# A decoder stack on one core: the barrier between the third feed-forward and the last self attention, and which engine casts the cross attention's keys

## The reference, cut to what matters

```python
x = x + _L2_ffn_ref(_layernorm(x), gate_w, gate_b, val_w, val_b, out_w, out_b)   # three bit_linear
x = x + _L3_attn_ref(_layernorm(x), w_qkv, b_qkv, w_out, b_out)                  # 16 heads of 16, causal
x = x + _L3_xattn_ref(_layernorm(x), ctx, mask, wq, bq, wk, bk, wv, bv, wo, bo)  # 16 heads of 16, int8 q and out
x = x + _L3_ffn_ref(_layernorm(x), ...)                                          # 7 experts, top 3, and a shared one

def bit_linear(x, w, b):
    scale_x = 127.0 / clip(max(abs(x), -1), 1e-5)
    x_dq = clip(round(x * scale_x), -128, 127) / scale_x
    gamma_w = clip(mean(abs(w)), 1e-5)
    return x_dq @ (clip(round(w / gamma_w), -1, 1) * gamma_w).T + b
# l2 ffn: bit_linear(silu(bit_linear(x, gate)) * bit_linear(x, val), out)
```

## Time and profile before

| | us |
|---|---|
| median of 3 runs | 1626.39 |
| lowest, highest | 1625.09, 1630.17 |
| the profiled execution | 1614.99 |
| its span | 1613.7 |
| PE busy, share of the span | 1374.7, 85% |
| DVE | 1080.9, 67% |
| ACT | 791.3, 49% |
| POOL | 757.0, 47% |

### The profile page before, as it was taken

How to read it: one execution, slowest core, us unless ns; L and a number is a source line. 1 busy time by engine, 2 the same in 40 slices (tenths; PEclk the granted TensorE clock), 3 DMA queues, 4 the chain that set the end, 5 groups by cost and what they waited for, 6 DMA issues and landing times. The chain is left out here.

```text
span 1613.7 us, 26001 instructions
## 1 busy us (share of the span) xinstructions
PE 1374.7 (85%) x8488; PEld 1038.5 (64%) x8488; DVE 1080.9 (67%) x2767; ACT 791.3 (49%) x2003; POOL 757.0 (47%) x1226
## 2 busy tenths in 40 slices
PE   6999997889999996777799698556888878889999
PEld 4666763578888872444477587424666655568887
DVE  7877786357767668898955736676766688853222
ACT  3444442144334357888821624456767668742111
POOL 4888882046666565777722122335556533320000
PEclk9999997999999998999999899869999999999999
DMA  8000001100000016656550000020423246310000
GB/s 291 15 8 8 1 1 68 56 15 8 1 8 1 1 11 127 111 100 108 102 209 1 0 1 0 4 111 14 66 50 57 43 96 168 75 14 1 7 8 13
DMA packets 177285, 79.98 MB, mean 50 GB/s; under 512 B 165376, under 2 KB 169856, under 8 KB 176000
## 3 DMA queue, kind: packets, MB, share of 16 engines
q1 hardware_dynamic: 177152, 78.33, 21.0%
HBM read 37.40 MB, written 1.05 MB: 24 GB/s over the span
## 5 line engine op out<-in xcount | busy, mean ns | idle before, releaser
L101 PE MATMUL banks<-normed_t,arena_a 128*128 128x256 f32 x1120 | 257.1, 385 | 2.5 <-PEq L3685 2.5
L464 POOL TENSOR_TENSOR lut_weights<-lut_weights,arena_b 128x536 f32<-128x536 f32 x128 | 181.3, 1417 | 123.6 <-DVE arena_b L454 114.4
L101 PEld LDWEIGHTS banks<-normed_t,arena_a 128*128 128x128 f32 x1120 | 215.2, 193 | 33.0 <-issue 3.1
L601 POOL TENSOR_SCALAR work<-work,small 128x256 f32<-128x256 f32 (+1 forms) x384 | 175.6, 475 | 37.1 <-DVE small L593 37.1
L1752 ACT ACTIVATE arena_a<-banks,work 128x1024 uint8<-128x1024 f32 x128 | 153.8, 1204 | 34.0 <-DVE work L1692 22.0
L1690 DVE TENSOR_REDUCE work<-banks 128x1 f32<-128x1024 f32 x128 | 155.5, 1215 | 11.8 <-PE banks L101 11.6
L1797 POOL TENSOR_SCALAR arena_a<-arena_a 128x1024 bf16<-128x1024 uint8 x128 | 132.4, 1045 | 57.4 <-DMA arena_a<-arena_a 54.9
L107 PE MATMUL banks<-identity,work 128*128 128x128 f32 x1000 | 140.0, 282 | 18.8 <-POOL work L601 7.2
L581 ACT ACTIVATE work<-banks,small 128x256 f32<-128x256 f32 (+1 forms) x258 | 114.8, 453 | 67.6 <-DVE small L568 55.4
L107 PEld LDWEIGHTS banks<-identity,work 128*128 128x128 f32 x1000 | 116.9, 145 | 41.6 <-issue 17.8
L1916 DVE TENSOR_TENSOR big_b<-big_b,banks 128x512 f32<-128x512 f32 (+2 forms) x48 | 30.8, 642 | 135.0 <-PE banks L101 122.8
(11 more groups left out here) (467 smaller groups left out, 3193.7 us busy)
## 6 DMA issues: line engine op xcount, KB each, us to landing
arena_a<-in_L3f_wg SPq DMA_DIRECT2D x8, 512.0 KB, 3.9
arena_b<-in_lut_idx SPq DMA_DIRECT2D x8, 268.0 KB, 3.3
arena_b<-in_L_wqn SPq DMA_DIRECT2D x4, 512.0 KB, 8.6
arena_b<-in_L_wo SPq DMA_DIRECT2D x4, 512.0 KB, 12.5
arena_a<-in_L_wq SPq DMA_DIRECT2D x1, 2048.0 KB, 7.5
arena_a<-in_L_wo SPq DMA_DIRECT2D x1, 2048.0 KB, 12.6
arena_a<-arena_a SPq DMA_TRANSPOSE x128, 2.5
arena_b<-in_L2f_gv SPq DMA_DIRECT2D x1, 2048.0 KB, 7.9
```

What stands on the lines that cost most here:

```text
L101: ins = t.matmul(out, lhs_t, rhs, start=start and i == 0, stop=stop and i == n - 1)
L464: g.tensor_tensor(o, o, lut_t[j % 2], ALU.add).then_inc(*summed.up(c * LUT + j))
L601: ins = g.tensor_scalar(e[:, c], e[:, c], A.rl[n % 2][:, 2 * hh + i:2 * hh + i + 1], 0.0, ALU.mult, ALU.add)
```

## The change

- `l2_ffn` has no meeting at its end. Steps 0 and 1 of self attention are issued in its steps 9 and 10, behind each engine's own work of the step; the common loop starts at step 2. `l3_attention()` is called once ahead of all stages.
- POOL's work behind the feed-forward's loop (masks, identity, fills, scaling) is issued in steps 3, 4 and 6; the value tiles' memsets in steps 6 and 8, three each.
- Batch 3's norm moves from steps 0 and 1 of self attention to step 5 (POOL), 6 (ACT) and 7 (PE's turn, ACT's copy).
- In place of the barrier there are waits: PE for the scaled weights and the last silu before projection 0, and before each score bank's first use; ACT for the last down product before the first exponentials, and for hidden tile 6 before the first query casts; DVE for hidden tile 7 before the first key casts.
- In cross attention POOL makes all the key casts (`key_parts_gpsimd`): the first behind the queries' bias, the second behind the rests of the first, both ahead of its own wait for ACT's cast, and the third at the start of the next even step, ahead of the next queries' bias. Self attention's key casts stay on DVE.

```diff
@@ exponentials_scalar
+            elif A.before:
+                a.wait_ge(*(yield A.before))
@@ l2_ffn, tensor (vector, scalar alike, in the loop over n)
-            yield MEET
+                if n >= NT + 1:
+                    yield from self_tensor(n - NT - 1)
@@ l2_ffn, gpsimd
-            for r in above:
-                g.memset(r, 0.0).then_inc(*gs.up())
...
-            yield MEET
+                if n == 3:
+                    for r in above:
+                        g.memset(r, 0.0).then_inc(*gs.up())
...
+                if n == 4:
+                    g.tensor_scalar(id_100, id_b, 100.0, 0.0, ALU.mult, ALU.add).then_inc(*gs.up())
...
+                if n == 6:
+                    g.wait_ge(*(yield loaded[9], "all"))
...
+                    gs.all("l3a", "scaled")
+                if n in (6, 8):
+                    half = narrow_vs[0:3] if n == 6 else narrow_vs[3:6]
+                    for r in half:
+                        g.memset(r, 0.0).then_inc(*gs.up())
...
+                if n >= NT + 1:
+                    yield from self_gpsimd(n - NT - 1)
@@ parts_vector, parts_scalar
+        if N is self_n and m < 2 and n == 0:
+            v.wait_ge(*(yield gs, "l2f", "hidden", NT - 1))
...
+        if N is self_n and m < 2 and n == 0:
+            a.wait_ge(*(yield h_in_psum, "l2f", NT - 2, 1))
+            a.wait_ge(*(yield gs, "l2f", "hidden", NT - 2))
@@ new
+    def key_parts_gpsimd(N, m, n):
+        cur, k5 = N.current(m, n), slots(N.kx[m % 2])
+        ks = K_SLOTS[n]
+        if n == 0:
+            g.wait_ge(*(yield vs, N.A.s, "keys", m))
+        else:
+            g.wait_ge(*rest_of.now())
+        for i in range(TB):
+            src = cur[:, i, 64:128].rearrange("p (h o c) -> p h o c", h=HG, o=1)
+            ins = g.tensor_copy(k5[:, i, :, ks[0]:ks[-1] + 1:3, :], src.broadcast_to([P, HG, len(ks), HD]))
+        ins.then_inc(*part_v.up(N.A.s, m, n))
@@ cross_parts_gpsimd
+        if m >= KEYS_BY_GPSIMD:
+            yield from key_parts_gpsimd(cross_n, m, n)
         yield from parts_gpsimd(cross_n, m, n)
@@ l3_attention, tensor
+                t.wait_ge(*(yield gs, s, "scaled"))
+                t.wait_ge(*(yield silued, "l2f", NT - 1, 1))
-            if n == 1:
+            if n == 7:
                 yield from norm_tensor(s, nf, heads_bank, [3], by_scalar=True)
@@ l3_attention, scalar
-            if n == 0:
+            if n == 6:
                 yield from norm_scalar(s, nf, None, [3], both=True)
@@ l3_cross, vector
-                if 0 < n <= UNITS and n % 2 == 0:
-                    yield from parts_vector(N, n // 2 - 1, 2)
...
-                    yield from parts_vector(N, n // 2, 0)
-                if n < UNITS and n % 2:
-                    yield from parts_vector(N, n // 2, 1)
@@ l3_cross, gpsimd
+                if 0 < n <= UNITS and n % 2 == 0:
+                    yield from key_parts_gpsimd(N, n // 2 - 1, 2)
```

More of the change, by code:

```diff
@@ L499, in __init__ @@
             self.qt = [w.take(q_cols, dt) for _ in range(2)] if q_cols else None
-            self.depth = depth
+            self.depth, self.before = depth, None
             self.after = turns_of.s if turns_of else None
@@ L2802, in gpsimd @@
                     yield from norm_gpsimd("l3a", [(n - 5) // 2])
-            for r in above:
-                g.memset(r, 0.0).then_inc(*gs.up())
[L2805 to L2815, removed]
+                if n == 3:
+                    for r in above:
+                        g.memset(r, 0.0).then_inc(*gs.up())
+                    g.wait_ge(*gs.now())
+                    for r, val in zip(above, (HUGE, -HUGE, MASKED / 100.0)):
+                        g.affine_select(out=r, in_=r, pattern=[[-1, P]], compare_op=ALU.is_ge,
+                                        fill=val, base=0, channel_multiplier=1).then_inc(*gs.up())
@@ new lines, in gpsimd @@
+                if n in (6, 8):
+                    half = narrow_vs[0:3] if n == 6 else narrow_vs[3:6]
+                    for r in half:
+                        g.memset(r, 0.0).then_inc(*gs.up())
+                    g.wait_ge(*gs.now())
+                    for r in half:
+                        g.memset(r.rearrange("p (h c) -> p h c", c=HS)[:, :, HD:HD + 1], 1.0).then_inc(*gs.up())
+                    gs.all("l3a", "ones")
+                if n >= NT + 1:
+                    yield from self_gpsimd(n - NT - 1)
@@ L3228, in gpsimd @@
         def gpsimd(n):
-            if n == 0:
-                for r in vs_:
-                    g.memset(r, 0.0).then_inc(*gs.up())
-                g.wait_ge(*gs.now())
-                for r in vs_:
-                    g.memset(r.rearrange("p (h c) -> p h c", c=HS)[:, :, HD:HD + 1], 1.0).then_inc(*gs.up())
-                gs.all(s, "ones")
+            if n == 5:
                 yield from norm_gpsimd(s, [3])
-                g.wait_ge(*(yield loaded[9], "all"))
             if 0 <= n - 5 < UNITS:
@@ L3400, in tensor @@
         def tensor():
-            for n in range(-AT, LAST):
+            for n in range(2 - AT, LAST):
                 yield from self_scores(n + AT)
```

22 lines of the change are left out of this document (16 added, 6 removed).

## The result

The changed kernel takes **1611.46 us** (median of 6 runs, 1610.05 to 1613.59) beside 1623.68 us for the kernel before in the same comparison (6 runs, 1620.34 to 1630.17). The ratio is 0.993, with a 95% interval of 0.990 to 0.996.

What follows compares the result with a forecast made beforehand. No engine bounds the whole; a chain of waits passes through several. Part 1's 3.3, casts' 1.7 and transposes' 1.8 sum to 6.8 us: 1608.2 from the profiled 1614.99, 1619.6 from the timed median 1626.39; range 1608 to 1627.

Steps and rivals of the forecast that it cites:

- rival A: Cross attention: the loop loosens more once VectorE sheds its casts; gain 10 to 18 us, chance 0.26.
- the transposes' terms: Cross attention: last pair's DMA wait goes, 2.2 us, smaller waits 0.7, 1.0 lost at residual adds; net given as 1.8.
- won at the first DMA: Feed-forward to self attention: without the barrier the first DMA transpose is issued at 1121.0 instead of 1125.3, 4.3 us won.
- lost in the fill: Self attention's fill: batch 3's norm on GpSimd ahead of the first shares delays pair 2's rests, 1.0 us lost.
- GpSimd's cast at 0.43 us: Cross attention: one 192-column key cast on GpSimd taken as 0.43 us, from a span of 0.37 to 0.81.
- casts 1.7: Cross attention's loop: VectorE's casts off the path win 1.6 and 0.6 us, later output integers cost 0.5; net 1.7 us.
- only the third stands in the loop: Cross attention: of a pair's VectorE key casts only the third lies on the loop's path, 0.27 us.
- a sign against it: Cross attention: the prediction is wrong if TensorE's heads keep waiting as long; no size given.
- The addition-laden pairs: Cross attention, once in four pairs: GpSimd's 1.28 us residual add precedes the third cast, ending 0.5 us later; 1.0 us lost.
- B: Cross attention gains nothing as GpSimd's casts delay other work; only the start's 3.3 us won, 1623; chance 0.22 with C.
- C: Start of self attention: removing the barrier wins 0, cross attention keeps 3.5 us, 1623; chance 0.22 with B.
- D: Cross pairs: GpSimd becomes the bound if a cast takes over 0.82 us; 20 us slower, 1646; chance 0.05.

Runs made afterwards that it cites:

- experiment 9: The changed kernel with GpSimd's part of batch 3's norm at the head of step 4, ahead of the rests; 1614.66 us, ratio 0.996 to the kernel before.
- experiment 6: The changed kernel with each cross key cast on GpSimd done twice; 1614.56 us, ratio 0.996 to the kernel before.
- experiment 8: The changed kernel with ScalarE's heads copy put first and all three cross key casts back on VectorE; 1613.71 us, ratio 0.996 to the kernel before.
- the casts alone: The kernel before, barrier kept, with the three key casts of each cross pair on GpSimd; 1617.62 us, ratio 0.998.
- the seam alone: The changed kernel with all three key casts of a cross pair back on VectorE; 1617.17 us, ratio 0.998 to the kernel before.
- Experiments 3 and 4: The changed kernel with only the first two (3) or only the third (4) cross key casts on GpSimd, the rest on VectorE; 1612.77 and 1611.50 us.
- experiment 7: The changed kernel with ScalarE's heads copy ahead of its wait for the next queries and their first casts; 1604.76 us, ratio 0.990 to the kernel before.

## Why the prediction was right, and where it was wrong

The sum was 6.8 us; at equal clock the gain is 8.0 ± 1.0. The verdict and the size held; the shown 12.2 us would have put it into rival A, and most of that excess is scatter of the median of before in that comparison (1623.68, 3.7 us above the median of 96). That the time came out 8 us below the predicted 1619.6 is mostly the median from which I started (1626.39, 6.4 us above it). The sum itself has a slip: the transposes' terms, 2.2 + 0.7 - 1.0, make 1.9 us, not 1.8. The 11.4 us by which that median stood over the profiled execution were a sign: 0.956 was among the highest clocks that this kernel gets.

*Part 1, won at the first DMA, 4.3 us.* Right: 4.7 in the traces.

*Part 1, lost in the fill, 1.0 us.* Right in place and nearly in size: 1.3 us, of which experiment 9 gives back 0.9. The lead over the kernel before is 4.7 us at the first pair's transposes and 3.4 at the third's, and it is still 3.4 at the eleventh (102.0 against 105.4): nothing is made up in the next pairs. At the twelfth it is 4.0 (109.0 against 113.0), as TensorE's wait for the transposes between 1200 and 1240 us fell from 1.7 to 1.0 us, and at the first cross pair 4.2 (4.5 and 4.1 in the other two traces). So **the term is mis-sized at the end of the stage**, not in the fill: part 1 is 3.3 us in my sum and 4.2 in the trace; 5.0 ± 1.5 timed agrees with the trace and hardly tells the two apart.

*Part 2, GpSimd's cast at 0.43 us.* 0.348 and 0.323, a fifth less. It cost little: by experiment 6 even twice that costs at most 0.3 us per pair.

*Part 2, casts 1.7 and transposes 1.8, together 3.5 us.* 2.9 ± 1.7 and 3.3 ± 1.6 were measured: the sum held. **The step "only the third stands in the loop" was not borne out**, at equal clock: the third alone kept 0.7 ± 2 of it, and the first two kept as much; that the sum held beside it is in part luck. VectorE's copy behind the first cast and ScalarE's heads copy were tied, and I took the tie as "worth nothing", where by the owners of the heads' wait and by experiment 8 the loop has more than one gate a fraction of a microsecond apart. The heads' wait changed its owner with the casts moved and did not shrink beside the kernel before (16.9 us, and 17.8, 17.8 and 16.6 in the change's traces), which the prediction had listed as a sign against it; with the casts alone moved it was 14.0, all on ScalarE's copy. What stays open is how the 3 us split among the three casts: both single moves lie within error of nothing and of most of it, and their ratios put the third cast alone higher than the fit does.

*The addition-laden pairs, 1.0 us lost.* The chain passes through the addition as I said; moving it brought 3.2 us in one trace and 1.6 ± 2.2 timed, so that the 1.0 us is neither shown nor excluded.

*Rivals.* A (the loop loosens by more) is excluded, at equal clock, for the change as it stands; when the copy went first the gain was of its size, 13.8 us. Its argument, DVE at 87%, named one of the two gates. B and C put the whole gain at 3.3 and 3.5 us and are excluded by the 8.0; the casts alone speak against B and the seam alone against C, each by the fit. D stayed far from its point of decision: 0.35 us against 0.82 for one cast.

## What to carry to other kernels

When a waits view puts nearly all of one wait on one engine, look for the second engine that would be late if the first were not: here the edit paid 3 us with ScalarE's copy where it stood, and 8 us with it put first. A loss or a lead found in the fill of a long pipeline should be followed pair by pair to the end of the stage, with the granted clock beside it: here a loss of 1.3 us stood for eight pairs, and the 0.9 us won back went beside a stretch of low clock. And where one trace of each kernel is compared, count positions from the last instruction ahead of the change, and read the granted clock of both spans before explaining a few microseconds.

## What the hardware showed beyond expectation

**The clock explains most of the scatter.** One program on one core took 1611.5 to 1631.4 us at mean granted clocks of 0.958 to 0.941 (1612.4 us at the highest of them, 1628.0 at the lowest). It can be seen in single stretches. Experiments 3 and 4 differ from the change only in cross attention, yet their first cross pair starts 2.6 us late (168.9 and 169.0 against 166.3). In both traces the granted clock is 0.83 between 1220 and 1230 us, within self attention, and 1.00 there in the changed kernel and in the one before. In the one with the first two casts on GpSimd the transposes of the thirteenth pair start at 124.0 us, in the changed kernel at 121.0. Chance alone is a weak reading of this. Of the 14 traces, four have a granted clock under 1.00 anywhere between 1150 and 1270 us: these two, both between 1220 and 1230, and the two with the norm moved, both between 1180 and 1192. The kernel before, the casts alone and the eight other traces of the changed seam have none. Nor are the stretches alike in cross attention: from 1300 to 1420 us the clock averages 0.95, 0.97 and 0.97 in the change's traces and 1.00 in that of experiment 7. Whether an edit changes the chance of such stretches was not tested, and the fit, which takes the clock as given, leaves such a gain or loss out.

**One cast on GpSimd hardly depends on its width, the second of two does.** 348 ns for 192 columns and 323 ns for 128. Two in a row take 0.64 and 0.53 us together, so the second adds 0.29 and 0.21 us. On VectorE, in the kernel before, the same pairs take 0.43 and 0.36 us where nothing disturbs them. The Trainium skill's "GPSIMD Engine Reference" (section "Engine selection") has GpSimd near line rate with one input and about twice as slow with two. Here, with one input, a pair took 1.5 times VectorE's time in both shapes.

**VectorE's casts are stretched beside GpSimd's additions.** In the fill of self attention the pair of casts took 1.43 us beside GpSimd's residual addition (1.30 in the earlier trace rows), where it takes 0.36 us otherwise. I had thought that this could be the 1.3 us lost in the fill; in experiment 9, with the norm moved, the pair still took 1.44 us, and most of the loss was won back.
